# Two transformer layers on one core: attention's first steps reordered around the layer norms, and a PSUM place changed for the second batch's scores

## The chip, the cores and the metric

One core of one Trainium2 chip runs the whole program in one launch. The metric is the device time of that execution in microseconds; before the change three runs gave 3593.13, 3593.5 and 3596.92 us, median 3593.5 us.

## The reference

```python
x = x + attention0(layernorm(x), ctx)      # x: 8 x 100 x 1024, ctx: 8 x 722 x 256, 16 heads
x = x + moe(layernorm(x))                  # 32 experts, top 4, width 512
x = x + attention1(layernorm(x), ctx)
x = x + ternary_ffn(layernorm(x))          # width 4096, weights quantised to -1, 0, 1
# attention: q_hk = x @ Wq.T; q_big = q_hk . w_kc_q (rope on it in layer 0 only)
#   q_r = q_big . W_qr; k_r = rope(ctx) . W_kr; softmax(q_r . k_r) @ rope(ctx) . w_kc_kv @ Wo.T
```

All of it is in float32 but the last block's products.

## The kernel before

The engines are programmed by hand: each has its own instruction list, and semaphores order them, so the order of work is the order of the calls in each engine's function. The 800 tokens lie in `X` as 7 tiles of 128 rows (the last has 32). The four phases are "a0", "moe", "a1" and "ffn" (lines 2218 to 2358 call them).

**Layer norm.** VectorE takes statistics (L432) set by set (`LN_SETS`), ScalarE the square root (L477), VectorE scales a tile into a room `hn` (L452, two rooms in both attention phases), TensorE transposes it with 8 instructions (L464), ScalarE copies it to `xnT` (L501). A tile needs a free room, so VectorE waits for the transposes of the tile two before it.

**Attention.** Heads go in 4 groups of 4 per layer (`hg`), both layers one after the other. In layer 0 a group starts with the query projections: `q_heads` (L785, 8 matmuls for each half of the 800 tokens), `q_big` (L802), rope on VectorE (`rotate`, L1289), `q_r_burst` (L817). The first group also prepares ctx: rope on VectorE (L553, L539) and GpSimd, transposes (L579), and writes kvT_d and kvN_d to memory. In layer 1 there is no rope on the query, so the weights of a pair of heads are multiplied first: `fold_m`, `fold_mt`, `fold_a`, `fold_at` (L833, L839, L850, L859), copied by ScalarE (`fold`), and `q_r1` (L869) applies the product to `xnT`. `u` is the pair, 0 or 1.

Then come 8 batches in each group (`for st in range(B - 1)` in `body`). Per batch TensorE does `scores` (L916, 6 row blocks `lc`, two at a time in a pair of PSUM banks that `score_bank` names, so three pairs), `keys` of a later batch (L890, two calls, `early` and `late`), `largest` (L991, transposes the maxima `mx`), `values` of the batch before (L931), the sum (L941) and `spread` (L999). ScalarE copies each pair of scores to `Sb` (L1184 for the first two, L1186 and L1187 for the third), copies the keys to `KR` (L1102), and takes the exponential (L1171) one batch behind. VectorE takes maxima (L1320, L1323, L1325), adds the negated maximum (L1335) and takes sums. In layer 1 ScalarE also sums the absolute values of the last block's weights, three pieces of 1024 columns a batch (`absolute`, L1128), which GpSimd loads in two rooms (L1439): a piece's load is issued once the piece two before it is summed.

The waits around the change: for batch 1, the third pair of scores used banks 0 and 1, those of the first pair, and waited for its copy; the early keys of batch 1's step use the same two banks and waited for all four copies:

```python
            return (0, 2, 0 if b == 1 else 4)[j]
                    pe.wait_ge(sem(f"{p}_se"), n_ev * hg + SEN * st + (2 if not u else SEN if st == 1 else 1))
                    elif lc == 4 and b == 1:
                        pe.wait_ge(sem(f"{p}_se"), n_ev * hg + SEN * b + 1)
```

**Between moe and a1.** SyncE's queue loads the first head pair's weights (`wq_h`, `wc_h`), waits until GpSimd has added the last expert's rows to memory (L1807, an accumulating scatter), and loads the sums `yl` (L1772). VectorE adds them to `X` and takes the norm. Then `first_loads` brings `wkr`, `kvT` and the next weights.

Of the kernel before, what the change touches and what calls it, by code (L numbers as in the profile page):

```python
# [168 lines left out]
def build(nc, A, stages=("a0", "moe", "a1", "ffn")):  # L169
    ctx = ExitStack()  # L170
    with ctx:
# [43 lines left out]
        phn0 = pa.here()  # L215
# [6 lines left out]
        psb0 = pa_sb.here()  # L222
        Sb = [pa_sb.put(f"Sb{i}", [P, LC, GW]) for i in range(2)]
# [175 lines left out]
        HN = {"a0": hn, "moe": hnm, "a1": hn, "ffn": hnf}  # L399
# [7 lines left out]
        LN_SETS = {"a0": ((0, 3), (3, MT - 1), (MT - 1, MT)), "moe": BEHIND, "a1": ((0, 4), (4, MT)), "ffn": BEHIND}  # L407
# [64 lines left out]
        def ln_scalar(eng, p, dst, pad=False):  # L472
# [17 lines left out]
            ahead = {"a0": (0, 1, 4), "moe": (MT, MT, 3), "a1": (0, 2), "ffn": (MT, MT, 2)}[p]  # L490
            for m in range(MT):
# [107 lines left out]
        def att_sync(sp, ly):  # L599
# [121 lines left out]
        def heads_bank(a, half, first):  # L721
            return 0 if first and a >= 1 else half
# [7 lines left out]
        def key_bank(ly, b, u, first=False):  # L730
            if ly == 0 and b < 2 and (b, u) != (1, 1):
# [6 lines left out]
        def fold_bank(u, n):  # L738
# [18 lines left out]
        def score_bank(b, j):  # L757
            return (0, 2, 0 if b == 1 else 4)[j]
# [14 lines left out]
        def att_tensor(pe, ly, parts):  # L773
# [53 lines left out]
            def fold_m(hg, u):  # L827
# [66 lines left out]
            def scores(hg, b):  # L894
                half, cols = b // BH, slice(b % BH * S, (b % BH + 1) * S)
                for lc in range(LC):
# [9 lines left out]
                    elif lc == 4 and b == 1:  # L906
                        pe.wait_ge(sem(f"{p}_se"), n_ev * hg + SEN * b + 1)
# [1451 lines left out]
```

## Time and profile before

| | us |
|---|---|
| median of three runs | 3593.5 |
| the profiled execution, its own time | 3597.0 |
| its span | 3595.3 |
| TensorE busy (PE) | 3454.1 (96%) |
| VectorE busy (DVE) | 1636.6 (46%) |
| ScalarE busy (ACT) | 863.0 (24%) |
| mean granted TensorE clock | 0.983 |

PE is TensorE's matmuls, PEld its weight loads, POOL GpSimd, SP SyncE. A row of the timeline gives start, busy time, engine, line, operation, output<-input, shape and count, and in brackets how long the engine was idle before it and what ended the wait. A float32 matmul is two records, so the 8 matmuls of half a `q_heads` are x16.

### The profile page before, as it was taken

What the parts mean: (1) busy time and instruction counts of PE and PEld (TensorE: products, weight loads), DVE (VectorE), ACT (ScalarE), POOL (GpSimd) and SP (SyncE); (2) the same over time, 40 slices, a digit from 0 to 9 for tenths busy, and PEclk for the clock granted to TensorE, in tenths of its full rate; (3) what the DMA queues carried; (4) which work ended last, traced back from release to release, by engine and by line L of the source; (5) the groups of instructions that cost most, each with busy time, mean ns of one, the idle gap of its engine ahead of it and who ended that gap; (6) DMA issues with size and microseconds to landing.
All of it is one profiled execution on the core that took longest, in us unless ns stands there. A gap on an engine that the chain in (4) does not pass through costs nothing.

```text
span 3595.3 us, 42917 instructions
## 1 busy us (share of the span) xinstructions
PE 3454.1 (96%) x16460; PEld 1810.2 (50%) x16461; DVE 1636.6 (46%) x1982; ACT 863.0 (24%) x1254; POOL 733.3 (20%) x697
## 2 busy tenths in 40 slices
PE   7899999999999789999999979999999999999999
PEld 4564565565456333333333346556565564554554
DVE  7764464565466531111111136436255275662661
ACT  2230131032023211111111125335144252220110
POOL 3200500400320012222222210000000002780760
PEclk9999999999999899999999989999999999999999
DMA  7631231132123295898879975436355251330320
GB/s 211 219 103 38 70 94 46 66 99 63 53 71 114 80 372 191 307 368 312 283 271 332 341 223 165 129 125 184 101 149 155 75 163 55 140 141 1 142 103 37
DMA packets 93027, 556.62 MB, mean 155 GB/s; under 512 B 11288, under 2 KB 11424, under 8 KB 74976
## 3 DMA queue, kind: packets, MB, share of 16 engines
q1 hardware_dynamic: 58288, 445.28, 34.9%
q0 software_dynamic: 31392, 93.76, 10.2%
q10 hardware_dynamic: 3216, 15.68, 1.4%
q8 instruction: 101, 1.65, 0.2%
q14 instruction: 30, 0.25, 0.0%
HBM read 517.62 MB, written 40.71 MB: 155 GB/s over the span
## 4 chain that ended last, share of the span: by engine, by line
PE 84%; DMA 6%; DVE 3%; ACT 2%; SPq 1%; issue 1%; POOLq 0%; DVEq 0%; POOL 0%; ACTq 0%
PE PS L931 14%; PE PS L1858 10%; PE PS L2177 10%; PE PS L1075 9%; PE PS L890 9%; DMA bias<-in_b 5%; PE PS L1882 5%; PE PS L2191 5%; PE PS L916 4%; PE PS L785 4%; PE PS L802 3%; PE PS L869 2%; PE PS L1013 2%; PE PS L817 2%; PE PS L941 1%; PE PS L1850 1%
## 5 line engine op out<-in xcount | busy, mean ns | idle before, releaser
L931 PE MATMUL PS<-Sb,kvN 121*128 121x400 f32 (+1 forms) x1536 | 538.4, 501 | 0.3 <-ACT Sb L1171 0.3
L1858 PE MATMUL PS<-W,hT 128*64 128x512 f32 x2208 | 508.8, 604 | 17.5 <-DMA bias<-in_b 15.2
L931 PEld LDWEIGHTS PS<-Sb,kvN 121*128 121x128 f32 (+1 forms) x1536 | 288.3, 191 | 206.6 <-issue 4.3
L890 PE MATMUL PS<-kvT,wkr 128*128 128x363 f32 x1024 | 347.0, 482 | 9.4 <-ACT Sb L1187 9.4
L2177 PE MATMUL PS<-xh,wq 128*128 128x400 f16 x2048 | 348.9, 334 | 0.9 <-DVE xh L1251 0.9
L1951 DVE TENSOR_TENSOR gu<-PS,bias 128x512 f32<-128x512 f32 x69 | 47.7, 692 | 641.3 <-PE PS L1858 641.3
L1075 PE MATMUL PS<-wb,ctxl 128*128 128x512 f32 x768 | 331.7, 594 | 4.2 <-ACT ctxl L1102 4.2
L2133 POOL TENSOR_SCALAR gtq<-stg,thr 128x1024 f16<-128x1024 f32 x96 | 290.1, 3037 | 183.3 <-DMA stg<-in_F 132.6
L1858 PEld LDWEIGHTS PS<-W,hT 128*64 128x64 f32 x2208 | 154.5, 139 | 310.5 <-issue 289.9
L1429 POOL TENSOR_TENSOR qrope<-qrope,rt 128x400 f32<-128x400 f32 x144 | 145.1, 1032 | 720.2 <-DVE rt L1289 720.2
L2177 PEld LDWEIGHTS PS<-xh,wq 128*128 128x128 f16 x2048 | 200.9, 98 | 148.9 <-issue 2.4
L1882 PE MATMUL PS<-W,actT 128*64 128x512 f32 x1104 | 250.4, 596 | 2.6 <-ACT actT L2006 2.6
L890 PEld LDWEIGHTS PS<-kvT,wkr 128*128 128x128 f32 x1024 | 188.7, 193 | 114.0 <-issue 19.9
L1075 PEld LDWEIGHTS PS<-wb,ctxl 128*128 128x128 f32 x768 | 145.7, 191 | 188.0 <-issue 179.4
L1335 DVE TENSOR_TENSOR Sb<-Sb,PS 121x2400 f32<-121x2400 f32 x64 | 169.9, 2654 | 94.1 <-PE PS L999 94.1
L1102 ACT ACTIVATE KR<-PS 128x726 f32<-128x726 f32 x128 | 99.3, 776 | 402.8 <-PE PS L890 402.8
L1389 DVE TENSOR_TENSOR X<-PS,X 128x512 f32<-128x512 f32 x96 | 66.4, 691 | 284.2 <-PE PS L1075 284.2
L916 PE MATMUL PS<-QR,KR 64*121 64x100 f32 x3072 | 181.2, 271 | 13.1 <-ACT Sb L1184 9.1
L916 PEld LDWEIGHTS PS<-QR,KR 64*121 64x121 f32 x3072 | 169.1, 183 | 47.8 <-issue 30.2
L785 PE MATMUL PS<-xnT,wq_h 128*128 128x400 f32 x512 | 185.4, 500 | 0.5 <-ACT xnT L501 0.5
L1351 DVE RECIPROCAL rz<-PS 128x400 f32<-128x400 f32 x64 | 169.6, 2650 | 24.4 <-PE PS L941 24.4
L2191 PE MATMUL PS<-wdq,hh 128*128 128x512 f16 x768 | 166.6, 380 | 0.0
(285 smaller groups left out, 3792.1 us busy)
## 6 DMA issues: line engine op xcount, KB each, us to landing
W<-in_W SPq DMA_DIRECT2D x96, 2048.0 KB, 12.0
stg<-in_F SPq DMA_DIRECT2D x32, 1536.0 KB, 6.3
kvT<-kvT_d SPq DMA_DIRECT2D x64, 726.0 KB, 4.3
kvN<-kvN_d SPq DMA_DIRECT2D x64, 726.0 KB
absin<-in_F POOLq DMA_DIRECT2D x48, 512.0 KB, 4.0
hn<-in_F POOLq DMA_DIRECT2D x48, 512.0 KB, 4.5
wb<-in_WB SPq DMA_DIRECT2D x8, 2560.0 KB, 9.1
wc_h<-in_WC SPq DMA_DIRECT2D x32, 576.0 KB, 5.8
```

Of the source, the lines that this page charges most:

```text
L785: mm = nc.tensor.matmul(PS[:, heads_bank(a, half, first), 0:HALF], wq_h[a % 2][:, c * K:(c + 1) * K], xnT[:, c, half * HALF:(half + 1) * H ...
L890: mm = nc.tensor.matmul(PS[:, bank + n, 0:LH], wkr[:, dc, u, w:w + P], kvT[b % 2][:, dc, n * LH:(n + 1) * LH], start=dc == 0, stop=dc == C ...
L916: mm = nc.tensor.matmul(PS[0:LP, bank + r, to:to + S], KR[b % 2][rows, u, lc * LP:(lc + 1) * LP], QR[rows, q, cols], start=True, stop=True)
L931: mm = nc.tensor.matmul(PS[:, value_bank(b) + dc, 0:GW], kvN[b % 2][0:k, lc, dc * P:(dc + 1) * P], Sb[b % 2][0:k, lc, :], start=lc == 0, s ...
L1075: mm = nc.tensor.matmul(PS[:, 2 + n % 4, :], ctxl[:, a, m * P:(m + 1) * P], wb[:, w:w + 512], start=a == 0, stop=a == HA - 1)
L1335: nc.vector.tensor_tensor(sb, sb, PS[0:LP, 5, 0:GW].unsqueeze(1).to_broadcast([LP, LC, GW]), ALU.add).then_inc(sem(f"{p}_sb"), 1)
L1351: nc.vector.reciprocal(rz[:, :], PS[:, z_bank(b), 0:GW]).then_inc(sem(f"{p}_rz"), 1)
L1858: mm = nc.tensor.matmul(PS[g * BS:(g + 1) * BS, 2 + u % 2, :], hT2[k][:, c, half * BS:(half + 1) * BS], W2[:, q, o:o + N1], start=c == 0, ...
L1882: mm = nc.tensor.matmul(PS[h * BS:(h + 1) * BS, 4 + u % 2, :], actT[:, j, g * BS:(g + 1) * BS], W2[:, u % NQ_W, o:o + DH], start=c == 0, s ...
L2133: nc.gpsimd.tensor_scalar(gtq[q][:, w, :], stg[q][:, w, :], thr[:, w:w + 1], None, ALU.is_gt).then_inc(sem("f_gt"), 1)
L2177: mm = nc.tensor.matmul(PS[:, 4 * q + 2 * w + half, 0:HALF], wq[q][:, w, c, :], xh[part][:, c, half * HALF:(half + 1) * HALF], start=c == ...
L2191: mm = nc.tensor.matmul(PS[:, n % 8, :], hh[part][:, c, m * P:(m + 1) * P], wdq[:, c, half], start=c == 0 and part == 0, stop=c == EB - 1 ...
```

## The change

It has five parts (`between(m)` below is TensorE's, called behind tile m's transposes; ScalarE has one like it with the copies). (1) In a0 the norm's sets are (0,2), (2,4), (4,7) rather than (0,3), (3,6), (6,7), it has six rooms, and the first half of the first head's `q_heads` stands between transposes. (2) ScalarE runs a one-column Exp before the groups of each layer, which brings its table load there. (3) In a1 `keys` of batch 0 stand ahead of the norm, with `wkr` and `kvT` loaded in the moe phase's SyncE list, and the second pair's folding and the first `q_r1` stand between the norm's transposes. (4) Batch 1's third score pair lies in banks 6 and 7, without its wait, and the early keys wait for one copy. (5) In layer 1 the third absolute sum of batch 0 is done in batch 1.

```diff
+        hn0 = [pln0.put(f"hn0{i}", [P, D]) for i in range(6)]
-        HN = {"a0": hn, "moe": hnm, "a1": hn, "ffn": hnf}
+        HN = {"a0": hn0, "moe": hnm, "a1": hn, "ffn": hnf}
...
-        LN_SETS = {"a0": ((0, 3), (3, MT - 1), (MT - 1, MT)), "moe": BEHIND, "a1": ((0, 4), (4, MT)), "ffn": BEHIND}
+        LN_SETS = {"a0": ((0, 2), (2, 4), (4, MT)), "moe": BEHIND, "a1": ((0, 4), (4, MT)), "ffn": BEHIND}
...
-            ahead = {"a0": (0, 1, 4), "moe": (MT, MT, 3), "a1": (0, 2), "ffn": (MT, MT, 2)}[p]
+            ahead = {"a0": (0, 0, 4), "moe": (MT, MT, 3), "a1": (0, 2), "ffn": (MT, MT, 2)}[p]
...
         def heads_bank(a, half, first):
-            return 0 if first and a >= 1 else half
+            return (0 if a >= 1 else 2 + half) if first else half
...
         def score_bank(b, j):
-            return (0, 2, 0 if b == 1 else 4)[j]
+            return (0, 2, 6 if b == 1 else 4)[j]
...
-                    pe.wait_ge(sem(f"{p}_se"), n_ev * hg + SEN * st + (2 if not u else SEN if st == 1 else 1))
+                    pe.wait_ge(sem(f"{p}_se"), n_ev * hg + SEN * st + (1 if u else 2))
...
-                    elif lc == 4 and b == 1:
-                        pe.wait_ge(sem(f"{p}_se"), n_ev * hg + SEN * b + 1)
...
+            def between(m):
+
+                if m == 3:
+                    if ly == 1:
+                        pe.wait_ge(sem(f"{p}_kre"), 2 * B * g0 + 2)
+                        fold_m(g0, 1)
+                    pe.wait_ge(sem("ln_ev"), ln_count(("a0", "a1")[ly], "ev", 4))
+                    if ly == 0:
+                        q_heads(0, 0, 0, range(0, KC // 2), True)
+                    else:
+                        q_r1(g0, 0, 0)
+                elif m == 4:
+                    if ly == 0:
+                        q_heads(0, 0, 0, range(KC // 2, KC), True)
+                    else:
+                        fold_mt(g0, 1)
+                        pe.wait_ge(sem(f"{p}_q1e"), 1)
+                elif m == MT - 1 and ly == 1:
+                    fold_a(g0, 1)
...
             if "fold" in parts:
                 fold_all(g0, 0)
+                keys(g0, 0, 0, first=True)
+                pe.wait_ge(sem("m_bda"), 2 * MT)
+                keys(g0, 0, 1, first=True)
...
                     if ly == 1:
-                        for w in range(2):
+                        for w in range(-1 if st == 1 else 0, 2):
                             absolute(hg, 3 * st + w)
...
-                    if ly == 1:
+                    if ly == 1 and st >= 1:
                         absolute(hg, 3 * st + 2)
...
+                eng.wait_ge(sem("m_bda"), 2 * MT + 2)
+                for u in range(2):
+                    c_key(g0, 0, u, True)
...
+            nc.scalar.activation(abpart[:, 0:1], cst[:, C_ONE:C_ONE + 1], ACT.Exp)
             for hg in range(g0, g0 + HG):
                 body(hg, first=hg == 0)
...
                 sp.dma_start(wc_h[a][:, :], A["WC1"][a]).then_inc(sem(f"a_wc{a}"), 16)
+            sp.dma_start(wkr[:, :, :, :], A["WKR1"][0].rearrange("p (c u n) -> p c u n", c=CC, u=HA // 2)).then_inc(sem("a_wr"), 16)
+            sp.wait_ge(sem("m_y"), last + 1)
+            sp.dma_start(kvT[0][:, :, :], kvT_d[0].rearrange("p (c l) -> p c l", c=CC)).then_inc(sem("a_kt0"), 16)
             sp.wait_ge(sem("m_fin"), 1)
```

On TensorE, at the start of the program (L464 and L467 are the norm's transposes, L785 and L794 `q_heads`, L802 and L811 `q_big`), before:

```order
L464 MATMUL PS<-cst_50,hn_107680_71 128x128 x8
L464 MATMUL PS<-cst_50,hn_111776_72 128x128 x8
L464 MATMUL PS<-cst_50,hn_107680_71 128x128 x8
L785 MATMUL PS<-xnT_59,wq_h_74368_60 128x400 x16
L802 MATMUL PS<-qhk_154144_84,wc_h_82560_62 128x400 x2
```

and with the change:

```order
L467 MATMUL PS<-cst_50,hn_119968_248 128x128 x8
L794 MATMUL PS<-xnT_59,wq_h_74368_60 128x400 x4
L467 MATMUL PS<-cst_50,hn_124064_249 128x128 x8
L794 MATMUL PS<-xnT_59,wq_h_74368_60 128x400 x4
L467 MATMUL PS<-cst_50,hn_128160_250 128x128 x8
L467 MATMUL PS<-cst_50,hn_107680_245 128x128 x8
L794 MATMUL PS<-xnT_59,wq_h_74368_60 128x400 x8
L811 MATMUL PS<-qhk_154144_84,wc_h_82560_62 128x400 x2
```

Half of the sixteen matmuls moved between the transposes of the last tiles.

On TensorE around the second norm (L899 `keys`, L878 `q_r1`, L848, L859, L868 the folding), with the change, first the end of the first pair's folding and the norm's first tiles, then what follows `fold_m` (L842, behind the fourth tile):

```order
L859 MATMUL PS<-wq_h_78464_61,m_sb_83 64x512
L868 MATMUL PS<-cst_50,aT_sb_98 128x128 x8
L899 MATMUL PS<-kvT_179744_93,wkr_66 128x363 x8
L467 MATMUL PS<-cst_50,hn_107680_71 128x128 x8
L467 MATMUL PS<-cst_50,hn_111776_72 128x128 x8
```

```order
L878 MATMUL PS<-xnT_59,a_sb_81 128x400 x8
L467 MATMUL PS<-cst_50,hn_107680_71 128x128 x8
L848 MATMUL PS<-cst_50,mT_sb_82 128x128
L467 MATMUL PS<-cst_50,hn_111776_72 128x128 x8
L467 MATMUL PS<-cst_50,hn_107680_71 128x128 x8
L859 MATMUL PS<-wq_h_74368_60,m_sb_83 64x512
```

Before, all seven tiles stood in a row and the keys came between `fold_a` and `fold_at` and behind `fold_at`.

On ScalarE in layer 1's first group, from batch 0's copies of scores on, before:

```order
L1128 ACTIVATE absin_64,abpart_58<-absin_64 128x1024
L1128 ACTIVATE hn_111776_72,abpart_58<-hn_111776_72 128x1024
L1102 ACTIVATE KR_122272_74<-PS 128x726
L1128 ACTIVATE absin_64,abpart_58<-absin_64 128x1024
L1184 ACTIVATE Sb_143520_77<-PS 121x800 x2
```

and with the change, where three sums stand behind batch 1's exponential and between its two key copies:

```order
L1224 ACTIVATE Sb_143520_77<-PS 121x800 x2
L1226 ACTIVATE Sb_143520_77<-PS 121x400
L1227 ACTIVATE Sb_143520_77<-PS,cst_50 121x400
L1211 ACTIVATE Sb_133920_76<-Sb_133920_76 121x2400
L1137 ACTIVATE KR_128096_75<-PS 128x726
L1163 ACTIVATE absin_64,abpart_58<-absin_64 128x1024
L1163 ACTIVATE hn_111776_72,abpart_58<-hn_111776_72 128x1024
L1163 ACTIVATE absin_64,abpart_58<-absin_64 128x1024
L1137 ACTIVATE KR_128096_75<-PS 128x726
```

## Rows read from the trace of the kernel before

**Rows 1.** PE's waits over the whole run: waited for: us in total, times, longest.

```profile
PE PS L890 <- ACT Sb L1187: 9.4, 8, 1.2
PE PS L916 <- ACT Sb L1184: 9.1, 4, 2.4
```

**Rows 2.** Windows from a batch's scores to its maxima: length, busy PE, PEld, DVE, ACT, POOL, PEclk, DMA, GB/s.

```profile
2416.53:2421.49 4.96, 4.96 (x56) 4.05 (x56) 4.45 (x5) 2.66 (x4) 0.53 (x1) 1.00 0.66 154
162.11:168.64 6.53, 5.26 (x57) 4.14 (x57) 5.21 (x4) 5.49 (x7) 0.00 (x0) 1.00 0.88 373
452.57:459.08 6.51, 5.25 (x56) 4.13 (x56) 5.21 (x4) 5.23 (x6) 0.00 (x0) 1.00 0.00 0
2162.56:2172.31 9.75, 6.69 (x56) 4.93 (x56) 4.80 (x4) 7.07 (x8) 0.53 (x1) 0.82 0.60 227
2393.63:2404.10 10.47, 6.94 (x56) 5.02 (x57) 4.79 (x4) 5.68 (x7) 0.53 (x1) 0.84 0.60 215
2857.24:2868.50 11.26, 7.68 (x56) 5.72 (x57) 4.79 (x4) 5.68 (x7) 0.53 (x1) 0.70 0.57 201
```

**Rows 3.** Timeline, layer 0, first group, batch 1, ScalarE.

```profile
166.29 1.28 ACT L1171 ACT_TABLE_LOAD   x1
```

**Rows 4.** Timeline, layer 1, second group: batch 0's maxima, then batch 1.

```profile
2389.69 0.62 PE L991 MATMUL PS<-cst,mx 121*100 121x121 f32 x4 [0.20 <-DVE mx L1325]
...
2396.00 1.06 ACT L1128 ACTIVATE absin<-absin 128x1024 f32<-128x1024 f32 x1 [2.42 <-DMA absin<-in_F]
...
2397.92 1.09 PE L916 MATMUL PS<-QR,KR 64*121 64x100 f32 x16 [2.35 <-ACT Sb L1184]
...
2400.19 4.37 PE L890 MATMUL PS<-kvT,wkr 128*128 128x363 f32 x8 [1.18 <-ACT Sb L1187]
```

**Rows 5.** The tile absin: how long its loads took.

```profile
DMA to landing us min/median/max: 3.7/4.0/9.9
```

**Rows 6.** Timeline of the start.

```profile
9.35 1.28 DVE L432 BATCH_NORM_STATS2 bn<-X 128x6 f32<-128x512 f32 x2 [0.99 <-DMA X<-in_x]
...
12.73 5.25 PE L464 MATMUL PS<-cst,hn 128*128 128x128 f32 x24 [12.73 <-DVE hn L452]
...
14.72 0.81 DVE L452 TENSOR_SCALAR hn<-X,mv,rstd 128x1024 f32<-128x1024 f32 x1 [1.40 <-PE PS L464]
...
23.11 0.81 DVE L452 TENSOR_SCALAR hn<-X,mv,rstd 128x1024 f32<-128x1024 f32 x1 [1.33 <-PE PS L464]
...
26.96 1.09 PE L464 MATMUL PS<-cst,hn 128*128 128x128 f32 x8 [1.34 <-DVE hn L452]
...
28.52 11.02 PE L785 MATMUL PS<-xnT,wq_h 128*128 128x400 f32 x32 [0.47 <-ACT xnT L501]
...
33.22 1.20 DVE L539 TENSOR_TENSOR crope<-crope,crot 121x512 f32<-121x512 f32 x1 [0.61 <-POOL crot L569]
...
40.92 0.99 DVE L1289 TENSOR_TENSOR qrope<-PS,ropeq 128x800 f32<-128x800 f32 x1 [6.50 <-PE PS L802]
```

**Rows 7.** Timeline around the second attention's norm, TensorE and one ScalarE row.

```profile
2110.15 4.46 PE L464 MATMUL PS<-cst,hn 128*128 128x128 f32 x24 [13.03 <-DVE hn L452]
...
2118.06 1.97 PE L464 MATMUL PS<-cst,hn 128*128 128x128 f32 x16 [2.06 <-DVE hn L452]
...
2136.28 2.72 PE L890 MATMUL PS<-kvT,wkr 128*128 128x363 f32 x8
...
2139.71 1.08 ACT L1102 ACTIVATE a_sb<-PS 128x512 f32<-128x512 f32 x2
```

**Rows 8.** Timeline of the last scatters and the sums read back.

```profile
2073.79 1.59 POOL L1807 DMA_INDIRECT acc_d<-ysb,sidxc  x1 [3.59 <-ACT ysb L2017]
...
2083.11 0.69 ACT L2017 ACTIVATE ysb<-PS,gcol 128x512 f32<-128x512 f32 x1 [7.98 <-DMA acc_d<-ysb,sidxc]
...
2094.61 1.23 DVE L1972 TENSOR_TENSOR X<-yl,X 128x1024 f32<-128x1024 f32 x1 [4.02 <-DMA yl<-acc_d]
```

**Rows 9.** DMA queues from 2076 to 2077 us: packets, MB, share of 16 engines.

```profile
q1 hardware_dynamic: 80, 0.27, 102.2%
```

More of the change, by code:

```diff
@@ L453, in ln_tile, with ln_tensor @@
                                     ALU.subtract, ALU.mult).then_inc(sem("ln_hn"), 1)
-        def ln_tensor(pe, p, then=None, fold=None):
+        def ln_tensor(pe, p, then=None, fold=None, between=None):
             for m in range(MT):
@@ L466, in ln_tensor @@
                 mm.then_inc(sem("ln_tp"), 1)
+                if between:
+                    between(m)
                 if then and m >= 1:
@@ L730, in key_bank @@
         def key_bank(ly, b, u, first=False):
+            if ly == 1 and first and (b, u) == (0, 0):
+                return 4
             if ly == 0 and b < 2 and (b, u) != (1, 1):
@@ L736, in lift_bank, with fold_bank @@
             return (3, 5)[n % 2] if more or n >= HA else n % 2
-        def fold_bank(u, n):
+        def fold_bank(u, n, first=False):
+            if first and u == 1 and n < 2:
+                return 2 + n
             return ((1, 0, 1, 0, 1, 0), (0, 1, 4, 5, 4, 5))[u][n]
@@ L952, in body @@
                     if first:
-                        for half in range(2):
-                            q_heads(hg, 0, half, range(KC))
+                        q_heads(hg, 0, 1, range(KC), first)
                     for a in range(HA):
@@ L975, in body @@
                 else:
[L976 to L984 removed]
+                    if hg == g0:
+                        q_r1(hg, 0, 1)
+                        fold_at(hg, 1)
+                    else:
+                        pe.wait_ge(sem(f"{p}_fe"), 12 * (hg - g0) + 6)
+                        fold_m(hg, 1)
+                        q_r1(hg, 0, 0)
+                        fold_mt(hg, 1)
+                        q_r1(hg, 0, 1)
+                        fold_a(hg, 1)
+                        keys(hg, 0, 0)
+                        fold_at(hg, 1)
+                        keys(hg, 0, 1)
                     for half in range(2):
@@ L1133, in body @@
                 if ly == 0:
-                    for half in range(2):
+                    for half in range(1 if first else 0, 2):
                         c_qhk(hg, 0, half, first)
@@ L1216, in body, with between @@
                     c_lift(n)
+            def between(m):
+                if ly == 0:
+                    if m == 4:
+                        c_qhk(0, 0, 0, True)
+                elif m == 3:
+                    fold(g0, 1, 0)
+                    c_qr1(g0, 0, 0)
+                elif m == 4:
+                    fold(g0, 1, 1)
+                elif m == MT - 1:
+                    for n in range(2, 4):
+                        fold(g0, 1, n)
             if "fold" in parts:
@@ L2263, in _ @@
                     att_scalar(eng, 1, ("fold",))
-                ln_scalar(eng, p, {"moe": hTm, "ffn": xh}.get(p, xnT), pad=p == "moe")
+                ln_scalar(eng, p, {"moe": hTm, "ffn": xh}.get(p, xnT), pad=p == "moe",
+                          between=att_scalar(eng, int(p[1]), ("between",)) if p[0] == "a" else None)
                 if p[0] == "a":
@@ L2291, in _ @@
                 ln_tensor(pe, p, then=(lambda m: logits(pe, m)) if p == "moe" else None,
-                          fold=(lambda ly: lambda: att_fold(pe, ly))(("moe", "ffn").index(p)) if p in ("moe", "ffn") else None)
+                          fold=(lambda ly: lambda: att_fold(pe, ly))(("moe", "ffn").index(p)) if p in ("moe", "ffn") else None,
+                          between=att_tensor(pe, int(p[1]), ("between",)) if p[0] == "a" else None)
                 if p[0] == "a":
```

57 lines of the change are left out of this document (30 added, 27 removed).

## The prediction

> **What bounds the kernel now.** I read the page first: TensorE is busy for 96% of the span, so only two things can move the time, work that goes away and moments in which TensorE stands. The change removes no matmul. So I went on to the waits of TensorE. Two of its lines belong to the edited code: the keys wait for the copy of the third score pair 8 times, 9.4 us in all, and the scores wait 4 times, 9.1 us in all, for the copy of the first pair [rows 1]. Eight is the number of head groups, four that of layer 1. Then the windows from a batch's scores to its maxima, with the clock [rows 2]. An ordinary batch (2416.53) takes 4.96 us. Batch 1 takes 6.53 and 6.51 in layer 0, and 9.75, 10.47 and 11.26 in layer 1, where the clock falls too: it is 0.70 to 0.84 in these windows and 1.00 in the others. Last the timeline at the two places where attention starts [rows 6, 7] and the scatters before the second [rows 8, 9].
>
> **Batch 1 in layer 0, 4 groups.** With banks 6 and 7 the third pair waits for no copy, and the early keys wait for the first pair's copy alone, which ScalarE ends while TensorE is at the third. TensorE is then through scores and keys in 4.96. What is late next is the maxima: VectorE must first end the shift of batch 0 and then needs the third pair's copy. The nearest row is batch 0's own maxima, for which TensorE waited 0.20 [rows 4]; in batch 1 the shift stands ahead of them, so I take 0.6, with 0 and 1.2 (the wait that goes, [rows 1]) as ends. That makes 5.55: 4 x (6.52 - 5.55) = 3.9 us. The Exp table load of 1.28 us stood between batch 1's copies and its exponential in the first group [rows 3]; now it runs while ScalarE waits for the second half of `q_heads`, some 5 us of TensorE, and costs nothing there. It was worth little, as the values that need the exponential come behind the maxima: 0.2 us. The Trainium skill (ScalarE: Activation LUTs, What ACT_TABLE_LOAD costs) puts a change of table at 2.66 us with the drain, which would make this 1.5 us; the next exponential began 1.28 us after the load did, so the trace doesn't show the drain. Term: **4.1**, ends 1.5 and 6.3.
>
> **Batch 1 in layer 1, 4 groups.** Here ScalarE stood 2.42 us in the third absolute sum of batch 0, because its load was not there, and the score copies stood behind it [rows 4]. So TensorE waited 2.35 for the first copy and 1.18 more for the keys' banks, and then ran the keys at half clock: 4.37 us for what takes 2.72 [rows 4, 7]. Moving that sum behind the exponential and removing the two waits takes all three away. The third group reads like the second, so before: 9.75 + 10.47 + 10.47 + 11.26 = 41.95 [rows 2]. After: 4 x 5.55 = 22.2. Term: **19.8**. Ends: 22.1 if the maxima are never late, 15.0 if 1.2 us more of waiting stays in each.
>
> The moved sum isn't free on ScalarE. Three sums of about 1.25 us now stand between batch 1's key copies, and the third's load can only be issued after the first of them. Counted from the start of the scores: third pair copied at 3.8, exponential to 6.0, key copy 0.8, first sum to 8.0, the load of the third 0.5 + 4.0 [rows 5] to 12.5, its sum to 13.8, late key copy to 14.6. Batch 2's scores need that copy at 5.55 + (2416.53 - 2404.10) = 18.0 [rows 2]. Slack 3.4 us, so I cost it at nothing.
>
> **Start of the program.** VectorE waited 1.40 and 1.33 us for transposes to free its two rooms and 0.99 for `X` [rows 6]. Six rooms end the first two, smaller sets hide the third, the work is the same: so the last tile, which TensorE took up at 26.96, is there 3.7 us earlier, at 23.2, and tile 4, two scalings of 0.8 before it, at 21.7. From tile 4 TensorE has three tiles of about 1 us, 2.7 us of `q_heads` between them, 0.6 for the last copy and hops, then the second half, 5.5 (half of 11.02): it ends near 33.9 where it ended at 39.5. That is 5.6 us at most. It needs the first quarter done by 21.7, and there the clock comes in: the first 24 transposes took 0.22 us each, the later ones 0.14 [rows 6], so TensorE starts at the lower level, and in the new order it is less busy early on. If it stays there, 16 transposes cost 1.3 us more and the first quarter 2.7, less the 0.7 in which TensorE would have waited for tile 4: the end slips by 3.3 us. I take **4.0**, between 2.3 and 5.6. VectorE paces the next 100 us, and its first rotation at 40.92 waited 6.50 us for TensorE; its own work ahead of that ends at 34.4 [rows 6]. So it can follow the whole way, and the gain holds.
>
> **Start of layer 1's attention.** Two keys, 2.4 us each, go from behind the norm into the 13.03 us in which TensorE waits for it [rows 7]: 4.8 us. Inside the norm TensorE waited 2.06 and about 0.8 in three small waits; `fold_m` and `q_r1` now stand there. Against it: a wait of about 1.3 for tile 3's copy (the gap of 2.06 and part of a copy, less 1.5 of `fold_m`), and about 0.8 before the next `q_r1`, since the copies of `a_sb` (1.08, [rows 7]) no longer lie beside keys. 4.8 + 2.9 - 2.1 = 5.6; counted instruction by instruction from tile 3 on I get 5.3. I take 5.4. Past SyncE's queue: `wkr` (0.39 MB) and `kvT` (0.74 MB) now stand ahead of the last scatter and the sums `yl`. The scatter issued at 2073.79 had landed by 2083.11, ScalarE stood 7.98 us for it, and VectorE later stood 4.02 us for `yl` [rows 8], so a delay there is a delay of the norm. The 1.13 MB at the 0.27 MB/us of [rows 9] would be 4.2 us if the scatters had to let all of it pass, and 0 if none. The scatter had room left behind its first packets, and `kvT` is nearly through when the last scatter starts: I take 1.0. The Trainium skill (DMA: Bandwidth & Descriptors, Queues, rings and completion order) says that a DMA engine takes turns between its queues, packet by packet. In [rows 9] SyncE's queue alone holds the engines, though the scatter had been issued; by the rule the cost would be some 0.4 us. Term: **4.4**, ends 1.2 and 5.6.
>
> **Sum.** 4.1 + 19.8 + 4.0 + 4.4 = 32.3 us. The profiled execution took 3597.0, which gives 3564.7; it is 3.5 above the median of the runs. On the median: 3593.5 - 32.3 = **3561.2 us**. The moe and ffn phases only move as a whole. The terms' ends add up to 20.0 and 39.6 us.
>
> **Rivals.**
> 1. *Both starts give nothing*: the clock stays low through the first norm, and the scatters pay for the loads. For it: 12.73's transposes at the lower level, the full queue. Against: 4.8 us of keys leave a stretch in which nothing hid them. 3593.5 - 23.9 = 3569.6.
> 2. *The keys' wait stays in another form*: the maxima, or the first pair's copy, come late by what the keys waited for. For it: VectorE's shift ahead of the maxima. Then layer 1 gives 15.0, layer 0 nothing: 23.4 us, 3570.1.
> 3. *Slower: the third sum's load in layer 1.* ScalarE takes its instructions in order. If that load takes 9.9 us as the longest did [rows 5], it eats the slack of 3.4 and 2.5 us more in each of 4 groups: 10 us, 3571. The sign turns only when four of them cost 32.3 us, 8 each, a landing of 15.5; past the measurement's bound it needs 17.3 us. At 20 us: (16.0 - 3.4) x 4 = 50.4, 3611.6. Median 4.0 speaks against it.
> 4. *The change doesn't act*: the waits removed were never last. [Rows 4] show TensorE released by them, so hardly. 3593.5.
>
> **Chances.** Forecast 0.68, the first rival 0.12, the second 0.10, the third 0.06 in its mild form and 0.02 with the sign turned, the fourth 0.02. A measurement of this kernel can tell about 0.2%, 7.2 us. Faster 0.95, same 0.03, slower 0.02. The range reaches from 3554 (the upper ends) to 3571, which takes in the first two rivals.
>
> **What would show it.** The two lines of [rows 1] are gone from TensorE's waits, or a wait for the maxima of about 0.6 stands there. The windows of batch 1 are 5.3 to 5.8 us in all 8 groups with the clock at 1.00. The first rotation stands at 35.5 to 38.6 instead of 40.92. Batch 0's first scores in layer 1 come some 4.4 us closer to the end of the last expert. Wrong it would be if the layer 1 windows stay above 7 us, if batch 2's scores wait for a key copy, or if `yl` comes more than 3 us later behind the last expert.

## The result, and the profile after

| | before | after |
|---|---|---|
| median of the runs, us | 3593.32 (4 runs, 3593.07 to 3596.92) | 3559.16 (4 runs, 3552.04 to 3559.41) |
| ratio of the two | | 0.9899, 95% interval 0.9887 to 0.9910 |
| the profiled execution's span | 3595.3 | 3557.5 |
| PE busy | 3454.1 | 3446.1 (97%) |
| mean granted clock | 0.983 | 0.987 |

The kernel is 34.2 us (1.0%) faster; 32.3 were forecast. 3559.2 stands against 3561.2, inside 3554 to 3571.

TensorE's waits after the change, whole run (waited for: us in total, times, longest):

```profile
PE PS L467 <- DVE hn L455: 19.3, 4, 10.4
PE PS L1001 <- DVE mx L1386: 6.9, 20, 2.1
PE PS L923 <- ACT KR L1137: 1.8, 4, 0.5
```

Both lines of [rows 1] are gone: neither `keys` (now L899) nor `scores` (L923) waits for a copy of `Sb`. The maxima (L1001) are in their place, with less than forecast: 5.3 us in 11 waits before, 6.9 in 20 now, and 0.15 to 0.20 us in the batches changed, where the forecast had 0.6. The windows of [rows 2] in the same order (ordinary batch; two of layer 0; groups 1, 2 and 4 of layer 1):

```profile
2389.92:2394.88 4.96, 4.96 (x57) 4.05 (x56) 4.45 (x5) 2.66 (x4) 0.53 (x1) 1.00 0.80 212
156.84:162.43 5.59, 5.44 (x58) 4.06 (x57) 5.21 (x4) 4.91 (x6) 0.00 (x0) 1.00 1.02 432
445.55:451.18 5.63, 5.43 (x58) 4.06 (x57) 5.22 (x4) 4.95 (x6) 0.00 (x0) 1.00 0.00 0
2145.43:2151.05 5.62, 5.42 (x56) 4.05 (x56) 4.79 (x4) 4.47 (x5) 0.00 (x0) 1.00 0.74 296
2372.12:2377.74 5.62, 5.43 (x56) 4.05 (x56) 4.79 (x4) 4.47 (x5) 0.00 (x0) 1.00 0.78 309
2825.43:2831.03 5.60, 5.45 (x57) 4.08 (x57) 4.79 (x4) 4.44 (x5) 0.00 (x0) 1.00 0.79 312
```

Batch 1 takes 5.6 us each time, at full clock. These five windows end where the maxima start. The windows of [rows 2] do not: 452.57 to 459.08 ends 0.31 us before the maxima (459.39), and the ordinary batch's, before and here, ends before the keys do, with the sum and then the maxima behind them. Read to the maxima like the new ones, batch 1 in layer 0 took 6.82 and takes 5.63:

```profile
459.39 0.58 PE L991 MATMUL PS<-cst,mx 121*100 121x121 f32 x4
...
2419.24 2.71 PE L890 MATMUL PS<-kvT,wkr 128*128 128x363 f32 x8
2421.80 0.84 PE L941 MATMUL PS<-sums,cst 121*128 121x400 f32 x2
```

Batch 1 of layer 1's second group, where [rows 4] had three stalls, then the moved work on ScalarE:

```profile
2372.12 2.79 PE L923 MATMUL PS<-QR,KR 64*121 64x100 f32 x48 [0.46 <-ACT KR L1137]
2374.83 2.71 PE L899 MATMUL PS<-kvT,wkr 128*128 128x363 f32 x8
2377.74 0.62 PE L1001 MATMUL PS<-cst,mx 121*100 121x121 f32 x4 [0.20 <-DVE mx L1386]
...
2389.92 2.26 PE L923 MATMUL PS<-QR,KR 64*121 64x100 f32 x38
```

```profile
2384.30 1.06 ACT L1163 ACTIVATE absin<-absin 128x1024 f32<-128x1024 f32 x1 [3.53 <-DMA absin<-in_F]
2385.26 0.19 ACT L1163 ACTIVATION_READ_ACCUMULATOR absin<-absin 128x1 f32 x1
2385.99 0.78 ACT L1137 ACTIVATE KR<-PS 128x726 f32<-128x726 f32 x1 [0.54 <-PE PS L899]
```

ScalarE still stands 3.53 us for a load, but nobody waits for it: the key copy ends at 2386.8, batch 2's scores take it at 2389.92. That is the 3.4 us of slack of the prediction, here 3.2.

Three lengths are used from here on, since they can be read in each profile to 0.1 us. The **step** is from batch 1's scores to batch 2's. The **start** is when batch 0's first scores begin in layer 0. The **a1 stretch** is from VectorE's first addition of `yl` to batch 0's scores in layer 1. Times worked out from PE's timeline:

```
           start    steps, layer 0              steps, layer 1              a1 stretch
before     153.04   19.53 18.95 18.96 18.95     22.18 22.90 23.00 23.69     58.39
after      147.76   17.78 17.80 17.80 17.78     17.80 17.80 17.80 17.78     52.62
gain         5.28    5.23 in all                20.59 in all                 5.77
```

The two profiled executions are 37.8 us apart in span. The four gains make 36.9; the way from the last expert to the first addition of `yl` took 1.55 more (20.94 for 19.39), and the moe phase, which the change leaves alone, 2.44 less (from batch 2's scores in layer 0's last group to the last expert: 1024.0 before, 1021.6 after). Over all fourteen profiles of this study that stretch is 1020.0 to 1025.6 us. So a whole time can't tell 3 us here, the lengths above can.

The rows of the start that answer to [rows 6]:

```profile
10.39 3.65 PE L467 MATMUL PS<-cst,hn 128*128 128x128 f32 x16 [10.39 <-DVE hn L455]
15.69 1.97 PE L467 MATMUL PS<-cst,hn 128*128 128x128 f32 x16 [1.65 <-DVE hn L455]
18.81 2.95 PE L794 MATMUL PS<-xnT,wq_h 128*128 128x400 f32 x8 [1.15 <-ACT xnT L506]
...
27.97 5.64 PE L794 MATMUL PS<-xnT,wq_h 128*128 128x400 f32 x16 [0.52 <-ACT xnT L506]
...
35.13 0.98 DVE L1350 TENSOR_TENSOR qrope<-PS,ropeq 128x800 f32<-128x800 f32 x1
```

The first 16 transposes take 0.23 us each, the next 0.12: TensorE went from half speed to full before the first `q_heads`. This is read from the durations, as the clock column says 1.00 for 10.39 to 14.04 too; in layer 1 of x12_fold_behind below, the same 16 transposes took 3.68 us at a granted clock of 0.50, as long as the 3.65 here. The rotation stands at 35.13 (40.92 before), a little ahead of the 35.5 to 38.6 that the prediction named as its sign.

### The profile page after: what moved, and what is told of

Its sections match the earlier page's. It is cut to its first block, busy times and chain, and to the rows that moved or that the text cites. A ratio compares the mean times of both kernels' runs of the same rounds, so it can differ in the third digit from the quotient of the medians.

```text
span 3557.5 us, 42921 instructions
## 1 busy us (share of the span) xinstructions
PE 3446.1 (97%) x16460; PEld 1800.4 (51%) x16461; DVE 1636.2 (46%) x1982; ACT 863.4 (24%) x1256; POOL 733.8 (21%) x697
## 4 chain that ended last, share of the span: by engine, by line
PE 84%; DMA 6%; DVE 4%; ACT 2%; SPq 1%; issue 1%; DVEq 0%; POOLq 0%; POOL 0%; ACTq 0%
PE PS L938 14%; PE PS L1922 10%; PE PS L2241 10%; PE PS L1085 9%; PE PS L899 8%; DMA bias<-in_b 5%; PE PS L1946 5%; PE PS L2255 5%; PE PS L923 4%; PE PS L794 4%; PE PS L811 3%; PE PS L878 2%; PE PS L1023 2%; PE PS L826 2%; PE PS L948 1%; ACT Sb L1224 1%
## 5 line engine op out<-in xcount | busy, mean ns | idle before, releaser
L938 PE MATMUL PS<-Sb,kvN 121*128 121x400 f32 (+1 forms) x1536 | 538.4, 501 | 0.0
L1922 PE MATMUL PS<-W,hT 128*64 128x512 f32 x2208 | 506.3, 601 | 17.4 <-DMA bias<-in_b 14.7
L938 PEld LDWEIGHTS PS<-Sb,kvN 121*128 121x128 f32 (+1 forms) x1536 | 287.5, 190 | 206.8 <-issue 4.1
L899 PE MATMUL PS<-kvT,wkr 128*128 128x363 f32 x1024 | 340.5, 475 | 0.0
L899 PEld LDWEIGHTS PS<-kvT,wkr 128*128 128x128 f32 x1024 | 185.0, 190 | 101.6 <-issue 3.7
L794 PE MATMUL PS<-xnT,wq_h 128*128 128x400 f32 x512 | 185.8, 500 | 1.7 <-ACT xnT L506 1.7
L923 PEld LDWEIGHTS PS<-QR,KR 64*121 64x121 f32 x3072 | 167.6, 182 | 37.1 <-issue 30.2
L923 PE MATMUL PS<-QR,KR 64*121 64x100 f32 x3072 | 178.4, 269 | 3.7 <-ACT KR L1137 1.8
```

The lines of the kernel that those rows point to most:

```text
L794: mm = nc.tensor.matmul(PS[:, heads_bank(a, half, first), 0:HALF], wq_h[a % 2][:, c * K:(c + 1) * K], xnT[:, c, half * HALF:(half + 1) * H ...
L899: mm = nc.tensor.matmul(PS[:, bank + n, 0:LH], wkr[:, dc, u, w:w + P], kvT[b % 2][:, dc, n * LH:(n + 1) * LH], start=dc == 0, stop=dc == C ...
L923: mm = nc.tensor.matmul(PS[0:LP, bank + r, to:to + S], KR[b % 2][rows, u, lc * LP:(lc + 1) * LP], QR[rows, q, cols], start=True, stop=True)
L938: mm = nc.tensor.matmul(PS[:, value_bank(b) + dc, 0:GW], kvN[b % 2][0:k, lc, dc * P:(dc + 1) * P], Sb[b % 2][0:k, lc, :], start=lc == 0, s ...
L1922: mm = nc.tensor.matmul(PS[g * BS:(g + 1) * BS, 2 + u % 2, :], hT2[k][:, c, half * BS:(half + 1) * BS], W2[:, q, o:o + N1], start=c == 0, ...
```

## Experiments

### The banks alone, the sum alone, both

On the kernel before, lines as in its listing. `x1_banks`:

```diff
-            return (0, 2, 0 if b == 1 else 4)[j]
+            return (0, 2, 6 if b == 1 else 4)[j]
-... SEN * st + (2 if not u else SEN if st == 1 else 1))
+... SEN * st + (1 if u else 2))
-                    elif lc == 4 and b == 1:
-                        pe.wait_ge(sem(f"{p}_se"), n_ev * hg + SEN * b + 1)
```

> The kernel before with the third score pair of batch 1 in banks 6 and 7 and the two waits shortened, the absolute sum left where it was. Theory (ScalarE's queue): in layer 0 the step from batch 1's scores to batch 2's falls from 18.95 to 17.8 us, 4.6 in all; in layer 1 the sum still holds the first pair's copy by 2.4, the keys now wait for that copy alone, and the step falls from 22.2-23.7 to about 20.2, 11 us in all: together 15.7, ratio 0.9956, 3577.6 us. Rival A (the banks were all of it, the sum's place is indifferent): 25 us, 3568. Rival B (TensorE still stands 2.4 us, so the clock falls as before): steps of 21.9 in layer 1, 9 us in all, 3584.

`x2_sum`:

```diff
-                        for w in range(2):
+                        for w in range(-1 if st == 1 else 0, 2):
-                    if ly == 1:
+                    if ly == 1 and st >= 1:
                         absolute(hg, 3 * st + 2)
```

> The kernel before with batch 0's third absolute sum moved behind the exponential of batch 1, banks and waits as before. Theory: layer 1 then reads like layer 0 before the change, step 18.95 with a keys' wait of 1.18 and the clock at 1.00; 91.8 - 4 x 18.95 = 16.0 us, ratio 0.9956, 3577.5 us. Rival A (the half clock comes from the keys' wait, too): steps of 20.6 and a clock below 0.9 in these windows, 9.4 us, 3584. Rival B (the load of the third sum now comes late and holds the copies of batch 2): a wait for a key copy in front of batch 2's scores.

`x3_both` has both edits.

> The kernel before with the banks, the two waits and the moved sum, but with both starts of attention and the Exp table as before. Theory: steps of 17.8 in seven groups and about 18.4 in the first group of layer 0, where the table load still stands; 5.2 - 0.6 + 20.6 = 25.2 us, ratio 0.9930, 3568.2 us. The two single edits give 15.7 and 16.0 together 31.7, so 6.5 us would be in both (either alone already keeps the clock up). Rival (the edits add up or help each other): 31 us or more, 3562.

| | ratio to before, interval | median us | steps, layer 0 | steps, layer 1 | gain in the steps |
|---|---|---|---|---|---|
| x1_banks | 0.9947 (0.9930 to 0.9963) | 3577.28 | 19.20, 17.80, 17.80, 17.78 | 20.74, 19.87, 19.88, 19.84 | 3.8 + 11.4 |
| x2_sum | 0.9954 (0.9937 to 0.9971) | 3578.6 | 19.54, 18.95, 18.95, 18.95 | 19.54, 18.96, 18.96, 18.96 | 0 + 15.4 |
| x3_both | 0.9926 (0.9910 to 0.9943) | 3568.95 | 19.20, 17.80, 17.80, 17.78 | 19.19, 17.81, 17.80, 17.78 | 3.8 + 19.2 |

The kernel before had 3596.29 on this chip. The medians moved by 19.0, 17.7 and 27.3 us, each more than the steps (15.2, 15.4, 23.0); the rest lies in stretches that these edits leave alone. In x1_banks, second group of layer 1, ScalarE's stall is as in [rows 4], and TensorE's keys wait for the first pair's copy (1.52 us), the maxima for VectorE (0.70):

```profile
2389.53 1.06 ACT L1126 ACTIVATE absin<-absin 128x1024 f32<-128x1024 f32 x1 [2.34 <-DMA absin<-in_F]
```

```profile
2391.55 2.68 PE L890 MATMUL PS<-kvT,wkr 128*128 128x363 f32 x8 [1.52 <-ACT Sb L1182]
2394.94 0.62 PE L989 MATMUL PS<-cst,mx 121*100 121x121 f32 x4 [0.70 <-DVE mx L1323]
```

In x2_sum the stall is gone and layer 1 reads to 0.01 us like layer 0 before:

```profile
2393.38 2.69 PE L890 MATMUL PS<-kvT,wkr 128*128 128x363 f32 x8 [1.18 <-ACT Sb L1187]
```

So both halves of the mechanism hold. The sum's stall is what made layer 1 differ from layer 0 (2.6 to 4.7 us a group with its half clock: the keys take 2.7 in both single edits, 4.37 in [rows 4]), the banks are worth the same 1.15 in both layers once it is gone. The single gains, 15.2 and 15.4, make 30.6, the two together 23.0: 7.6 us are counted twice, 1.9 a group. Most of that is the half clock, which either edit alone avoids: 1.7 us in the keys of the second group, where the clock is 1.00 in both single edits. Missed was the group with the table load, 19.20 instead of 18.4, in both layers. That led to the next one.

### The table load

`x4_table_late` is the changed kernel without the early Exp.

```diff
-            nc.scalar.activation(abpart[:, 0:1], cst[:, C_ONE:C_ONE + 1], ACT.Exp)
```

> The changed kernel without the early Exp activation. Theory: the first group's step from batch 1's scores to batch 2's in layer 0 is 18.4 instead of 17.8 (0.6 of the 1.28 us load), nothing elsewhere: 3559.8 us. Rival A (my term): 0.2 us. Rival B (the Trainium skill's 2.66 us for the change with its drain): 2 us in the first group of each layer, step 19.8, 3563.

Ratio 0.9899 (0.9882 to 0.9915), 3559.37 us. First group's step 19.21 in layer 0 and 19.20 in layer 1, 17.8 in the other six: 1.4 us in each layer, 2.8 in all. The total can't show that, the steps do. My 0.2 and the 0.6 both fall, and so does the 2 us of rival B. ScalarE, then TensorE:

```profile
162.62 1.28 ACT L1211 ACT_TABLE_LOAD   x1
163.92 2.20 ACT L1211 ACTIVATE Sb<-Sb 121x2400 f32<-121x2400 f32 x1
```

```profile
164.37 0.62 PE L1001 MATMUL PS<-cst,mx 121*100 121x121 f32 x4 [0.15 <-DVE mx L1385]
166.17 4.30 PE L938 MATMUL PS<-Sb,kvN 121*128 121x400 f32 x12 [1.19 <-ACT Sb L1211]
```

`values` (L938) comes right behind the maxima and waits for the exponential. Before, the keys' wait covered half of the load; with that gone the whole 1.28 lies on the path. The Trainium skill (ScalarE: Activation LUTs, What ACT_TABLE_LOAD costs) has 2.66 us for the change; the exponential starts 1.30 after the load does, and the cost is 1.4, so the trace again shows no drain.

### The start in layer 0, in halves

`x5_heads_behind`: the changed kernel with `q_heads` behind the norm. `x6_old_norm`: with the old sets and two rooms.

```diff
# x5
-                        q_heads(hg, 0, 1, range(KC), first)
+                        for half in range(2):
+                            q_heads(hg, 0, half, range(KC), first)
# and between(m) empty for layer 0
# x6
-        LN_SETS = {"a0": ((0, 2), (2, 4), (4, MT)), ...
+        LN_SETS = {"a0": ((0, 3), (3, MT - 1), (MT - 1, MT)), ...
-        HN = {"a0": hn0, ...
+        HN = {"a0": hn, ...
```

> The changed kernel with the first heads' matmuls of layer 0 behind the whole norm again (six rooms and the smaller sets stay). Theory (TensorE has idle stretches between the tiles that the first half filled): the norm ends near 24.5, then 11.0 us of heads, so the first rotation stands at 37.5 instead of 35.1 and batch 0's first scores 2.4 us later, 3562. Rival (smaller sets did it all, TensorE would have been as early without the moved half): 35.1, no loss. Rival (clock): with less work early TensorE stays at half clock longer and the rotation slips to 39.

> The changed kernel with the norm's sets and the two rooms of before in layer 0 (the first half of the heads stays between the tiles). Theory: the last tile is again there at 27, so 27 + 1.1 + 0.5 + 5.6, with the second quarter squeezed in before it: the first rotation at 37 to 38.5 instead of 35.1, loss 2 to 3 us, 3562. The gains of the two halves then add up to the 5.3 us of both. Rival (either alone gives it all): 35.1.

| kernels | first rotation | start |
|---|---|---|
| the four with the old start | 40.7 to 41.9 | 153.0 to 155.1, mean 153.9 |
| the eight with the whole new one | 35.1 to 36.6 | 147.7 to 150.3, mean 148.9 |
| x5_heads_behind (3557.32, ratio 0.9897, 0.9881 to 0.9914) | 39.10 | 151.8 |
| x6_old_norm (3565.29, ratio 0.9917, 0.9900 to 0.9933) | 41.87 | 155.3 |

The halves, one profile each against groups that spread over 2.1 and 2.6 us, don't add up. The norm alone gives about 2.1 of 5.0 us, the moved heads on top of it 2.9. The moved heads without the norm gain nothing: x6 stands at the slow end of the old start, 1.4 us behind its mean. In x5 the last three tiles' transposes ran partly at half clock after a longer idle stretch (0.18 us each, granted clock 0.66), so the clock rival, which said 39, was right there in part; in x6 the first quarter of `q_heads` itself did (clock 0.59), 4.98 us for 2.95:

```profile
21.98 4.21 PE L467 MATMUL PS<-cst,hn 128*128 128x128 f32 x24 [4.31 <-DVE hn L455]
```

```profile
24.05 4.98 PE L794 MATMUL PS<-xnT,wq_h 128*128 128x400 f32 x8 [1.11 <-ACT xnT L506]
```

With the whole new start the clock is not certain either: the second 16 transposes took 1.97 to 2.11 us in three of the eight kernels (and in x5), 3.38 to 3.68 in the other five. The first rotation stood at 35.33 in the mean of the three and at 36.08 in that of the five, the start at 148.0 and 149.4. So up to the rotation the low clock goes with 0.75 us, where I had feared 3.3. The 1.4 at the start may hold more than the clock: from rotation to start the fourteen profiles take 112.1 to 113.8 us, whatever the transposes did.

### The start in layer 1

`x7_keys_only`: the changed kernel with the keys ahead of the norm, but `fold_m`, `fold_mt`, `fold_a` and the first `q_r1` behind it.

> The changed kernel with layer 1's two keys ahead of the norm, but fold and q_r1 behind it again. From VectorE's first addition of yl to batch 0's first scores it was 57.6 to 58.4 us in the kernels with the old start and 52.6 and 52.9 in those with the new one. Theory: the keys give 4.8, less 0.8 for the copies of a_sb: 53.2 to 54.0, total 3559 to 3561. Rival (the keys only move a wait, the work between the tiles gives the gain): 56 or more, 3563.

3562.25 us (3559.59 without its longest execution), ratio 0.9905 (0.9885 to 0.9925); that one of the four took 18680.4 us, which nothing in the profiled one explains, and which stays open. a1 stretch 54.01. The old order has 57.64 to 58.39, mean 58.0, in four profiles, the new 52.2 to 52.9, mean 52.4, in six. So the keys give 4.0, as worked out, and the work between the tiles 1.6: 5.6 for the 5.4 of the forecast.

`x8_load_more` puts one more load ahead of the last scatter:

```diff
+            sp.dma_start(kvT[1][:, :, :], kvT_d[1]...).then_inc(sem("a_more"), 16)
             sp.wait_ge(sem("m_fin"), 1)
```

> The changed kernel with one more load of 0.74 MB (the second key tile, fetched a second time later) in SyncE's queue ahead of the last scatter. From the last scatter but one to yl's first addition it took 19.8, 19.9, 20.8 and 22.1 us in four kernels without the early loads (1.13 MB) and 19.9 to 22.4, mean 21.4, in six with them: 0.7 more. Theory (the engines take the scatter's packets in turn, the loads cost it tenths): 0.5 us for 0.74 MB more, so 21.9, total 3559.7. Rival (the scatter and the sums stand behind the whole queue): 0.74 MB at 0.3 MB/us, 2.5 us, so 23.9, total 3561.7.

3559.65 us, ratio 0.9899 (0.9882 to 0.9915). From the last scatter but one to the first addition: 21.57 us. With the single loads it is 21.5 in the mean of nine profiles (19.9 to 22.5), without any 20.7 in the mean of four (19.8 to 22.1). So 1.13 MB cost 0.8, within the spread, and 0.74 MB more cost nothing seen at VectorE in the one profile. One link does show the extra load. From the last scatter to SyncE's issue of `yl`, which waits for it, thirteen profiles have 4.5 to 5.05 us and this one 6.21:

```profile
2074.70 1.57 POOL L1874 DMA_INDIRECT acc_d<-ysb,sidxc  x1 [1.17 <-ACT ysb L2084]
```

```profile
2080.91 3.38 SPq L1839 DMA_DIRECT2D yl<-acc_d  x7
```

The changed kernel has 4.86 in that link and the one before 4.87: in the changed one the scatter's queue has the engines to itself from 2073 us on (94.9% of them, the loads' queue 0.1%), so `kvT` is through when its packets come. In x8 they meet, and the traces show the two queues side by side. First x8 from 2077 to 2078 us, then the kernel before from 2080 to 2081 (q1 the loads, q0 the scatter; packets, MB, share of the engines):

```profile
q1 hardware_dynamic: 50, 0.23, 54.7%
q0 software_dynamic: 35, 0.07, 54.2%
```

```profile
q0 software_dynamic: 53, 0.11, 58.3%
q1 hardware_dynamic: 52, 0.19, 50.3%
```

So the rival (the whole queue first, 2.5 us) falls, and the 102.2% of [rows 9] was a microsecond in which the scatter had no packets out. The kernel before has none of that queue from 2075 to 2079 us. Why they come so late stays open. What makes `yl` itself take 4.9 to 7.3 us from issue to addition, with and without the early loads, stays open.

### The slower rival, made to happen

`x9_late_load` delays the load of the third sum between batch 1's key copies:

```diff
+                        if (st, w) == (1, 1):
+                            for i in range(12):
+                                ...
+                                nc.gpsimd.tensor_tensor(junk[:, :], cst[:, 0:256], cst[:, 0:256], ALU.add).then_inc(sem("ab_more"), 1)
                         pool.dma_start(absin[k % 2][:, :], src[:, w * D:(w + 1) * D]).then_inc(sem(f"ab_in{k % 2}"), 16)
```

> The changed kernel with twelve scratch additions on GpSimd, about 9 us, in front of the load of the third absolute sum between batch 1's key copies, in all 4 groups of layer 1. Theory (ScalarE in order; the late key copy has 3.9 us of room: the sum ended at 2158.5 and may end at 2162.4 before batch 2's scores wait): the step from batch 1's scores to batch 2's grows from 17.8 by 9 - 3.9 = 5.1 us, 20 us in all, 3580. Each us less of delay is 4 us less in total. Rival A (the slack of 3.4 that I worked out is much too small, since the next batches absorb it): under 10 us in all. Rival B (none left, another wait was hidden just behind): 36 us, 3595.

3590.43 us, ratio 0.9990 (0.9980 to 0.9999): nearly all of the gain is eaten. The steps of layer 1 are 22.75, 22.90, 23.76 and 22.73, 4.95 to 5.96 longer for the 5.1 worked out. But the next steps, batch 2 to 3, are 20.57, 19.77, 21.22 and 19.68 instead of 17.4: 11.6 us that I had not counted. Timeline, first group of layer 1, GpSimd, ScalarE, TensorE:

```profile
2153.64 9.06 POOL L1504 TENSOR_TENSOR junk<-cst 128x256 f32<-128x256 f32 x12 [8.13 <-ACT absin L1164]
```

```profile
2166.82 1.06 ACT L1164 ACTIVATE absin<-absin 128x1024 f32<-128x1024 f32 x1 [12.24 <-DMA absin<-in_F]
```

```profile
2168.69 5.20 PE L924 MATMUL PS<-QR,KR 64*121 64x100 f32 x48 [4.79 <-ACT KR L1138]
2173.82 3.47 PE L900 MATMUL PS<-kvT,wkr 128*128 128x363 f32 x8
```

Behind the 4.79 us wait the scores take 5.20 for 2.79 (granted clock 0.50) and the keys 3.47 for 2.71 (0.77): these 3.2 us are what the next step is longer in this group. A delay of 9.1 us costs 32.6. With the usual landing of 4.1 that is a landing of 13.2, and it eats nearly what the change gives; I had put that point at 15.5. In the changed kernel the loads took 3.7, 4.1 and 9.5 (min, median, max), and all four steps are 17.8, so none of the long ones ate the slack.

### Further: smaller sets in layer 1 too

TensorE still stood 7.13 us for layer 1's first scaled tile. `x10_sets1`: sets of 2, 2 and 3; the first square root ahead of the key copies; `fold_m` behind tile 1.

> The changed kernel, further: layer 1's norm in sets of 2, 2 and 3 tiles, its first deviation ahead of the key copies, fold_m behind tile 1. TensorE stood 7.1 us for the first scaled tile. Theory: q_r1 then starts at tile 3's copy 5.6 us earlier and everything behind it follows: from yl's first addition to the scores 47 instead of 52.7, total 3553.5. Rival A (VectorE becomes the bound: two more small steps and tile 6 late): 50, 3556.5. Rival B (the clock falls in the idle stretches and stays down): no gain.

3557.71 us, ratio 0.9896 (0.9880 to 0.9913), a1 stretch 56.84, 4.4 longer. VectorE and GpSimd:

```profile
2090.80 5.67 DVE L455 TENSOR_SCALAR hn<-X,mv,rstd 128x1024 f32<-128x1024 f32 x2
2096.39 3.37 DVE L2040 TENSOR_TENSOR X<-yl,X 128x1024 f32<-128x1024 f32 x1
```

```profile
2090.80 7.87 POOL L1908 TENSOR_TENSOR X<-yl,X 128x1024 f32<-128x1024 f32 x3 [15.23 <-DMA yl<-acc_d]
```

Two scalings take 5.67 us for 1.53 while GpSimd adds. `x11_dve_adds` keeps x10's edits and gives VectorE all additions of `yl`:

```diff
-            for m in range(4, MT):
-                pool.wait_ge(sem(f"m_cg{m // 2}"), 16 * min(2, MT - m // 2 * 2))
-                nc.gpsimd.tensor_tensor(X[0:TW[m], m, :], yl[m][0:TW[m], :], X[0:TW[m], m, :], ALU.add).then_inc(sem("m_addp"), 1)
```

> The kernel with layer 1's norm in sets of 2, 2 and 3 tiles, and the last three additions of yl on VectorE instead of GpSimd. With them on GpSimd two scalings took 5.67 us where they take 1.53 alone, and the next addition 3.37 instead of 1.21, and the scores came 56.8 us after yl's first addition. Theory (the two engines were in each other's way, 6.3 us): VectorE's three additions cost 3.6 but the 6.3 go; tile 3 is copied at 18.2 us after yl's first addition, q_r1 follows at once, 48 us to the scores, total 3554.5. Rival (the two scalings are long for another reason, such as TensorE's transposes): still 56 or more.

```profile
2087.70 1.53 DVE L455 TENSOR_SCALAR hn<-X,mv,rstd 128x1024 f32<-128x1024 f32 x2
2089.14 1.22 DVE L2035 TENSOR_TENSOR X<-yl,X 128x1024 f32<-128x1024 f32 x1
```

3553.62 us (3552.63 to 3555.8), ratio 0.9889 (0.9872 to 0.9905), a1 stretch 49.2, 3.2 shorter than the changed kernel's mean and 7.6 shorter than x10's. `x12_fold_behind` is the same with `fold_m` behind tile 3.

> The kernel with layer 1's norm in sets of 2, 2 and 3 and all additions of yl on VectorE, but fold_m again behind tile 3, as in the changed kernel. Behind tile 1 it waited 4.35 us for its weights' load and ran at half clock until 2097.7, while the third scaled tile was there at 2096.0. Theory: tile 2's transposes start 1.7 us earlier and fold_m lies beside tile 3's copy, so the scores come 47.6 us after yl's first addition instead of 49.2, total 3552.2. Rival (fold_m costs 2.8 us at half clock behind tile 3, and gives back what was won): 49 to 50.

3559.78 us, ratio 0.9900 (0.9883 to 0.9916), a1 stretch 49.9. The rival holds:

```profile
2104.74 2.62 PE L844 MATMUL PS<-wc_h 128*64 128x128 f32 x24
```

`fold_m` takes 2.62 at half clock on the path. Its total is 6 us above x11's, yet the a1 stretch accounts for 0.7 only; 4.3 lie in the moe stretch (1024.3 against 1020.0), where the two do the same. So x11_dve_adds is the best kernel, and 3.2 us better than the changed one by the a1 stretch; the totals, 3553.6 and 3559.2, agree but could not show it.

## Why the prediction was right

- **Batch 1, layer 0**: 4.1 forecast, 5.2 measured (ends 1.5 and 6.3). The window came out at 5.6 for the 5.55 forecast, and that is luck: two errors cancel. Scores and keys take TensorE 5.4 us, not 4.96, since the ordinary window in [rows 2] ends before the keys do, and the maxima wait 0.15 to 0.20, not 0.6, as VectorE ends that close behind the keys. The time before was read 0.3 short by the same kind of window, so the banks give 1.15 us in each group where the table load isn't, for the 0.97 forecast. And the Exp table was mis-sized: 0.2 forecast, 1.4 measured once the keys' wait is gone. "The values that need the exponential come behind the maxima" was true and proved nothing, as they come at once behind them.
- **Batch 1, layer 1**: 19.8 forecast, 20.6 measured (15.0 to 22.1), of which 1.4 belongs to the table load that I had only placed in layer 0. The other 19.2 rest on the same short windows. The cause (the sum's load, ScalarE's order, the half clock) is shown by x1_banks and x2_sum.
- **Slack of the late key copy**: 3.4 worked out, 3.2 read in the second group. x9_late_load gives 3.1 to 4.1, group by group (9.1 of delay less the 4.95 to 5.96 seen), so the slack is real and of that size. What a miss costs was wrong: I priced each us over the slack at one us a group, and the wait also took the clock down for the next scores.
- **Start of the program**: 4.0 forecast, 5.3 in the two profiles, 5.0 in the means (2.3 to 5.6). VectorE followed nearly the whole way, as argued: its first rotation came 5.8 us earlier, the scores 5.3. Where the clock stays low early, as in five of eight kernels, 0.75 is missing at the rotation.
- **Start of a1**: 5.4 forecast ahead of the loads, 5.6 measured; for the loads 1.0 was taken and 0.8 is seen, within the spread. Net 4.8 for 4.4 in the means; in the two profiles 5.77 less 1.55, so 4.2. The Trainium skill's taking turns (DMA: Bandwidth & Descriptors, Queues, rings and completion order) would have given 0.4. The queues' shares above, 58.3 and 50.3% in one microsecond, agree with taking turns; the times fit 0.4 as well as 1.0 and exclude the 4.2 of the full queue.
- **Rivals**: both starts give something, so the first falls; the second falls with the windows of 5.6; the third's mild form didn't occur; the fourth was never near.

The terms measured make 35.6 against 32.3, all four a little above their forecast; the medians are 34.2 apart, and the moe stretch alone moves by more than that difference. That the total came within 2.0 us of the forecast is partly luck.

## What to carry to other kernels

An in-order engine that also does background work should do it behind the copies that another engine waits for, and its loads should be issued early enough for that place; price a miss at the wait plus the half clock that follows it. Windows that are to be compared must end at the same instruction: the ones here ended 0.3 us apart, and the forecast per group was 0.97 for 1.15. When a wait is removed, look at once for what it covered: here a table load worth 0.6 us became worth 1.4. And where a phase that the change doesn't touch moves by 5 us between executions, judge small edits by lengths in the trace.

## What the hardware showed beyond that

- **VectorE beside GpSimd.** While GpSimd added `yl`, two scalings took 5.67 us for 1.53 and an addition 3.37 for 1.21 (x10); without GpSimd's additions they were back (x11). In the changed kernel two instructions met them: an addition, 2.50 for 1.21, and the small one that ends the statistics (L448), 1.80 for 0.16 in x11. Together that is 2.9 us on the way to the first scaled tile, close to the 3.2 by which x11 is better, though x11 has smaller sets too:

```profile
2095.80 1.80 DVE L448 SCALAR_TENSOR_TENSOR shift_n<-mv,rstd 128x4 f32<-128x4 f32 x1
```

The Trainium skill (SBUF — State Buffer, Who interferes with whom) says that such instructions hold a shared port exclusively and the other blocks until the end. The trace of x10 agrees: GpSimd's three additions ended at 2093.15, 2095.91 and 2098.68, and the two scalings and the addition that met them 0.55, 0.56 and 1.08 us after that, at 2093.70, 2096.47 and 2099.76.
- **The clock after a pause.** The same 16 transposes of layer 1's tiles 2 and 3 took 3.68 us behind a pause of 4.17 (x12, granted clock 0.50) and 3.26 in x11, behind a `fold_m` that was itself at half clock (0.50) after a pause of 4.35; at full clock 16 of them take 1.94.
- **The moe phase** took 1020.0 to 1025.6 us in fourteen profiles of the same work. Its waits for the experts' biases and its half-clock matmuls differ from one to the next: at 1611.55 the kernel before ran one block in 5.35 us at a granted clock of 0.68, behind a wait of 2.04; the changed one ran it in 3.65, behind 1.63. What decides it stays open.
